# Decoder layer on one core: TensorE's order inside an attention step

## What is computed

```
x = x + attn(layernorm(x))            # ranks of 64, cumulative sums over the tokens
x = x + xattn(layernorm(x), ctx)      # causal softmax attention over own tokens and context
x = x + ffn(layernorm(x))             # FP4 quantised gate, up, down; inner width 704

# xattn
normed = rmsnorm(hidden); v_pool = concat(normed, ctx)
q = normed @ q_w.T; k = v_pool @ k_w.T
attn = softmax(mask(q @ k.T / 16)); h = attn @ v_pool
alpha = sigmoid(hidden @ gate_w.T + gate_b)
return (1 - alpha) * hidden + alpha * h
```

## Time and profile before

| | us |
|---|---|
| median of three runs | 540.25 |
| lowest and highest run | 540.16, 540.3 |
| the profiled execution | 540.15 |
| its span, first to last instruction | 538.4 |
| PE busy in the span | 521.7 |
| DVE busy | 451.3 |
| POOL busy | 410.9 |
| ACT busy | 342.8 |

### The profile page before, as it was taken

One profiled execution on the slowest core, in us unless ns is written; L12 is line 12 of the kernel. 1 busy time (PEld: TensorE's weight loads), 2 busy tenths in 40 slices (PEclk: granted clock), 3 DMA queues, 4 the chain that ended last, 5 costly groups with the idle time before them and its releaser, 6 DMA issues.

```text
span 538.4 us, 10582 instructions
## 1 busy us (share of the span) xinstructions
PE 521.7 (97%) x3084; PEld 454.9 (84%) x3084; DVE 451.3 (84%) x1118; ACT 342.8 (64%) x811; POOL 410.9 (76%) x639
## 2 busy tenths in 40 slices
PE   8898899999999999999999998999999999999996
PEld 5777788888888888888888886998899999999996
DVE  3798889777897867969589689998899999999886
ACT  3555844737437474563675767787788888888763
POOL 4267939859589497697787937889988888888854
PEclk9999999999999999999999999999999999999999
DMA  8720500000000000000000000000000000000001
GB/s 234 214 80 2 162 0 2 0 2 1 1 1 0 2 0 2 2 0 1 1 2 2 0 1 1 11 19 19 13 22 22 21 20 19 19 19 19 21 19 50
DMA packets 16130, 13.86 MB, mean 26 GB/s; under 512 B 3883, under 2 KB 15839, under 8 KB 16095
## 3 DMA queue, kind: packets, MB, share of 16 engines
q1 hardware_dynamic: 16095, 13.43, 8.0%
HBM read 9.23 MB, written 4.19 MB: 25 GB/s over the span
## 4 chain that ended last, share of the span: by engine, by line
PE 72%; DVE 15%; issue 6%; ACT 4%; POOL 1%; DVEq 0%; ACTq 0%; POOLq 0%
PE ps L1062 16%; PE ps L1064 15%; PE ps L1063 15%; PE ps L1265 10%; PE ps L1453 3%; PE ps L1253 2%; PE ps L1263 2%; DVE parts L1541 2%; PE ps L1184 1%; PE ps L1401 1%; DVE X L1606 1%; PE ps L1313 1%; DVE gz L1627 1%; DVE xn_sums L1571 1%; DVE st L1612 1%
## 5 line engine op out<-in xcount | busy, mean ns | idle before, releaser
L1062 PE MATMUL ps<-keys_h,nT_h 128*128 128x256 f32 (+6 forms) x272 | 85.8, 315 | 1.4 <-DVE keys_l L1541 1.0
L1063 PE MATMUL ps<-keys_l,nT_h 128*128 128x256 f32 (+6 forms) x272 | 83.1, 306 | 0.0
L1064 PE MATMUL ps<-keys_h,nT_l 128*128 128x256 f32 (+6 forms) x272 | 83.1, 305 | 0.0
L1062 PE MATMUL ps<-parts,xq_parts 128*128 128x512 f32 (+1 forms) x192 | 74.6, 388 | 0.0
L1064 PE MATMUL ps<-parts,xq_parts 128*128 128x512 f32 (+1 forms) x192 | 72.0, 375 | 0.0
L1063 PE MATMUL ps<-parts,xq_parts 128*128 128x512 f32 (+1 forms) x192 | 71.8, 374 | 0.0
L1265 PE MATMUL ps<-V,probT 128*128 128x256 f32 x288 | 67.4, 379 | 0.0
L774 ACT ACTIVATE prob<-ps,nbias 128x205 f32<-128x205 f32 (+7 forms) x32 | 25.7, 803 | 61.9 <-DVE nbias L1633 61.8
L1265 PEld LDWEIGHTS ps<-V,probT 128*128 128x128 f32 x288 | 54.6, 190 | 7.6
L1062 PEld LDWEIGHTS ps<-keys_h,nT_h 128*128 128x128 f32 x272 | 51.3, 189 | 5.8 <-DVE keys_l L1541 1.2
L1063 PEld LDWEIGHTS ps<-keys_l,nT_h 128*128 128x128 f32 x272 | 51.3, 189 | 3.2
(11 more groups left out here) (236 smaller groups left out, 1594.1 us busy)
## 6 DMA issues: line engine op xcount, KB each, us to landing
X<-in_x_dram SPq DMA_DIRECT2D x8, 512.0 KB, 4.6
out_dram<-X SPq DMA_DIRECT2D x32, 128.0 KB, 1.7
early<-in_L_ffn_w_down_dram SPq DMA_DIRECT2D x1, 704.0 KB, 6.9
early<-in_L_ffn_w_gate_dram SPq DMA_DIRECT2D x1, 640.0 KB, 4.5
early<-in_L_ffn_w_up_dram SPq DMA_DIRECT2D x1, 640.0 KB, 5.8
ctx_rows<-in_ctx_dram SPq DMA_DIRECT2D x1, 308.0 KB
early<-in_L_attn_Winv_dram SPq DMA_DIRECT2D x1, 256.0 KB, 3.8
early<-in_L_attn_WQ_dram SPq DMA_DIRECT2D x1, 256.0 KB, 3.6
```

The lines of the kernel that those rows point to most:

```text
L1062: mm(o, wh, mh, start=start, stop=False, **kw)
L1063: mm(o, wh, ml, start=False, stop=False, **kw)
L1064: return mm(o, wl, mh, start=False, stop=stop, **kw)
```

## The change

Only PE's `batch` is changed. Within a step the order was: logits, turns of tile i-1, projections (third and fourth), gates, ..., values of tile i-2. It becomes: logits, projections (third and fourth), gates of steps 4 and 6, values of tile i-2, turns of tile i-1, and the rest as before. `y_half(b+1, 0)` keeps its place after the logits of step 5. The first two projections of a half (steps 3 and 6) stay behind. The gates of steps 0 and 1 stay where they were. No instruction is added or removed, and no other engine's order changes.

```
--- before.py
+++ after.py
@@ -1331,8 +1331,17 @@
                         logits_tile(b, i)
                     if is_first(b) and i == 0:
                         keep_warm(FIRST_WARM, 4)
+                    if more and i == 4:
+                        proj_tiles(b * 2 + 2, (2, 3))
                     if more and i == 5:
                         y_half(b + 1, 0)
+                    if more and i == 7:
+                        proj_tiles(b * 2 + 3, (2, 3))
+                    if i in (4, 6):
+                        for t in GATES[i]:
+                            gate_tile(b, t)
+                    if i >= 2:
+                        pv_tile(b, i - 2)
                     if not more and i == TPB:
                         turn_tile(b, TPB - 1, (0, 1))
                         pe.wait_ge(s_w_h, 2 * KD)
@@ -1344,10 +1353,6 @@
                     elif 1 <= i <= TPB and not (is_first(b) and i == 2):
                         turn_tile(b, i - 1)
                     if more:
-                        if i == 4:
-                            proj_tiles(b * 2 + 2, (2, 3))
-                        if i == 7:
-                            proj_tiles(b * 2 + 3, (2, 3))
                         if i == TPB:
                             turn_nrm(b + 1, 0)
                             turn_nrm(b + 1, 1)
@@ -1356,7 +1361,7 @@
                         if not is_first(b):
                             turn_nrm(b, 2)
                             turn_nrm(b, 3)
-                    if not (i == 0 and is_first(b)):
+                    if i == 1 or (i == 0 and not is_first(b)):
                         for t in GATES[i]:
                             gate_tile(b, t)
                     if i == 1 and is_first(b):
@@ -1376,8 +1381,6 @@
                         gate_up(0, 0, 2, first=True)
                         turn_wd(2)
                         x_turn(2)
-                    if i >= 2:
-                        pv_tile(b, i - 2)
                     if i == 2 and is_first(b):
                         keys_products(b, 1)
                         logits_tile(b, 3)
```

More of the change, by code:

```diff
@@ L1346, in batch @@
                     if more:
[L1347 to L1350, removed]
                         if i == TPB:
```

## The result

| | before | after |
|---|---|---|
| median, us | 540.2 | 556.47 |
| lowest and highest run | 539.66, 540.3 | 555.57, 557.33 |
| span of the profiled execution | 538.4 | 555.5 |
| mean granted clock of TensorE | 1.000 | 0.994 |

The changed kernel is slower: the ratio is 1.0302, 95% interval 1.0285 to 1.0319. The forecast was 552.4 with a range of 545.6 to 556.8. The direction and the range hold; the size is 16.3 us instead of 12.2. The profiled execution is the slowest of the four after the change (557.33), so what is read from its trace adds up to more than the medians say. In the execution of 557.16 us the mean clock was 0.997, in the other three 0.994. The lines of `batch` and of DVE's `mix_tile` stand 3 lines lower after (`dmix` is L1646, `h_chunk` L1752).

The account below looks back on a forecast made before the run. TensorE, busy for 97% of the span, was taken as the bound, so reordering could win little. 540.15 + 4.5 (three edges) + 7.7 (last batch) = 552.35, called 552.4 us; 80% range 545.6 to 556.8.

Parts of the forecast that it names:

- The gains of steps 5 and 6: Steps 5 and 6: PE gaps of 0.43 and 0.30 us go, 0.73 us for each of three batches, 0.28 in the last.
- These edits cost nothing: Steps 2 to 7: nothing new waits for the exponentials, and the logits hide ACT's copies; no cost.
- The edges: Step 8 between batches: new waits of 1.0 us before values of tile 6, 1.2 before tile 7; net +1.5 us each.
- ACT's last copy takes 0.59 us: Step 8: turns of tile 6 done on PE at 245.2, so the turned tile is ready at 245.9.
- term of 4.5 for three edges: Step 8 of three batches: net shift of +1.5 us each, gains of steps 5 and 6 inside, +4.5 in all.
- The gap of 3.65 us: Last batch: PE idle from 312.7 to 316.35, before the values of tile 7; at about 317 with the edges' 4.5.
- the clock rival: Last batch: clock falls in the long gap, values of tile 7 cost 3.7 us more, 556.1 us; chance 0.08.
- gaps of 1 us leave the pace as it is: Argument against the clock falling in the 3.65 us gap expected in the last batch.
- the chain argument: Start of the FFN: its serial chain waits for the second gate/up product, so the whole chain moves by 7.7 us.
- without a pause: Start of the FFN: DVE was busy with the serial chain unbroken until `h_chunk` of the next tile at 322.29.
- the 1.4 us of draining: ScalarE's table load before the first silu: skill adds about 1.4 us per switch; the forecast used the row's 1.28 us.
- one of 7.7: Last batch, steps 8 and 9: second gate/up product starts at 320.05 instead of 312.31, +7.7 us; bounds 4.1 to 7.7.

Follow-up runs that it names:

- the body alone: Against the kernel before: only steps 2 to 7 in the new order, steps 8 and 9 in the old one, in all batches; 541.39 us, ratio 1.0029.
- the old edge: Against the kernel after: values of tile 6 behind `y_half(b+1, 1)` again in the first three batches; 551.21 us, ratio 1.0206.
- The values moved alone: Against the kernel before: only the values of tile 7 of the last batch moved ahead of the gate/up products; 544.55 us, ratio 1.0082.
- the kernel with the last values behind: Against the kernel after: values of tile 7 of the last batch back behind the two gate/up products; 549.68 us, ratio 1.0188.
- the early mix: Against the kernel after: DVE's reciprocal and `dmix` of tile 6 at the head of its step 8, batches 1 to 3; 555.71 us, ratio 1.0283.
- twelve products: Against the kernel after: twelve extra 128x512 matmuls, output unread, ahead of the last batch's values of tile 7; 554.84 us, ratio 1.0280.
- four products: Against the kernel after: four extra 128x512 matmuls, output unread, ahead of the last batch's values of tile 7; 557.06 us, ratio 1.0313.
- The two kernels with only the body changed: Against the kernel before: steps 2 to 7 in new order, 541.39 us; the same with step 7's turns of tile 6 back behind the logits, 538.08 us.

## Why the prediction was right or wrong

**The gains of steps 5 and 6.** Predicted 0.73 us in each of three batches and 0.28 in the last; measured 0.70 and 0.26 to 0.30. Right, and the kernel with the body alone shows them without the rest. "These edits cost nothing" was not quite right: about 0.2 us a batch are lost between tiles 0 and 5, in part behind `gz`. What was missed besides is what the body does to step 8, 0.71 us per batch if the values do not lie between: the paragraph named the exponentials and the copies as possible waits, not the banks of the turns. In the kernel after it does not bind, so the sum was not hurt by it. It is the main reason why two experiments (the old edge, the body alone) came out otherwise than expected.

**The edges.** Both waits were predicted with place and size: 1.0 us ahead of the values of tile 6 (measured 0.94), 1.2 ahead of those of tile 7 (1.17), 6.0 us between `y_half` and the latter by my count (251.9 to 257.9; measured 5.97). The releaser of the first is ACT, not DVE. The mix ended 0.47 us before the copies, although I had them 0.3 us the other way. The term that was sized too small is "ACT's last copy takes 0.59 us": three copies stand in a row there, and from 248.74 to 249.87 they take 1.13 us. The values of tile 6 then took 3.53 us instead of 3.27, and those of tile 7 3.80 instead of 3.71, since they start behind a pause. Together an edge costs 2.76 where 1.5 + 0.73 = 2.23 was said. The sum's term of 4.5 for three edges was in truth 6.66 (-0.94 to 5.72 in the table), the losses between tiles 0 and 5 included.

**The end of the last batch.** The gap of 3.65 us was predicted at about 317 and measured as 3.48 at 319.5. Its place moved by the edges' excess and by 0.9 us of late copies, slower values and drift. The values then took 6.82 us instead of 3.71. This is the clock rival, which I had given 0.08, and it came true on top of the forecast with 3.1 us, the largest single miss. The step that failed is "gaps of 1 us leave the pace as it is", taken as evidence against for a gap of 3.65 us, when the nearest row, the 442 ns per product behind 2.1 us without work, was evidence for it. A price with such a row behind it belonged into the sum. The Trainium skill ("TensorE: Matmul & The Clock Gate", What's actually happening) says that an idle TensorE is throttled to half its clock, and the trace agrees: 0.50 from 323 to 327 us.

**Nothing is given back.** "If the gap at the end is there but the FFN ends less late, the chain argument is wrong": the x turn at 333.1 is 17.51 us late. PE hardly waits behind it and makes up 3.5 us of that by the one at 337.6 (14.05), but then it waits 2.49 us for `h_chunk`, and from the x turn at 345.2 to the end the kernel is 17.2 us late. The values moved alone (544.55) show the same with a gap of 0.63 us. The argument from the rows was a little too strong (DVE was not wholly "without a pause", it waited 0.23 us at 319.07), but the conclusion held. The table load and the silu stand in the trace after as they stood before (the copies end at 320.20, the load starts at 320.22 and takes 1.28 us, the silu starts at 321.51), so the 1.4 us of draining did not appear here either.

**The sum, with what was measured.** -0.94 in the preparation, +6.66 for three batches with their edges, -0.08 inside the last, +8.3 for the order of step 9 (3.1 of it the clock), +3.25 for the order of step 8: 17.2 us. Against my 12.2 the trace misses 5.0: 3.1 for the clock, 2.2 at the edges, 0.7 in the rest of the tail, less 1.0 from the preparation and inside the last batch. I had counted the last two terms as one of 7.7, and that there are two was learned from the kernel with the last values behind: it removes the gap and still keeps 3.25. Nor do the two simply add up: alone they cost 4.5 (the values of tile 7 moved in the kernel before) and 3.25 us, together 11.5, because the 3.48 us gap and the slow values behind it arise only where both meet.

That the range holds is partly luck. The forecast's sum left the clock's price out, the range's upper bound lies 0.3 us above the median, and the profiled execution (557.33) lies outside it, although its preparation was 0.94 us shorter.

## What to carry to other kernels

On this saturated engine moving work cost next to nothing by itself; what counted is who waits behind the moved piece, and in which order that engine's own queue serves it. Ask for each piece: does another engine's serial chain start here, and what did the piece that used to stand between two others cover (a bank, a copy, a mix)? And where a gap like the 2.6 and 3.5 us here is forecast on TensorE, put the slower matmuls behind it into the sum, not only the gap.

A wait that is removed on a busy engine can return a little later if its suppliers have not moved: the early mix took away three waits of 1.17 us, and the median fell by 0.8 us (555.71 against 556.47).

## What was not expected of the hardware

- The granted clock fell with idle times of 2.49 us (values moved alone), 2.50 us (twelve products), 2.62 us (four products) and 3.48 us (kernel after), and stayed at 1.00 with two of 2.49 us (340.50 in the kernel after, 340.27 with four products). The length of the gap does not tell these apart, and what else decides is open.
- Where it fell in the kernel after, it was 0.50 while PE worked without a pause from 323 to 327 us, and it was 1.00 from 330 us on. Behind the 2.62 us gap it fell only about a microsecond after the work had begun.
- A fall of the clock cost 3.1 us where a chain waited behind the slow matmuls, and nothing at the end where PE had to wait a little later anyway (the two gaps of 2.49 and 2.50 us).
- Twelve like matmuls at the start took between 4.12 and 5.30 us in executions of the same instructions, so one trace's end can be off by 1.2 us through that alone. The two kernels with only the body changed differ from before by 2 us or less, so they are judged by several runs and by the milestones in between.
